# Decoder block with routed experts on one core: the row scatters of late attention steps issued one by one between GpSimd's splits and sums, or together

## The chip, the cores and the metric

The kernel runs on one core of a Trainium2 chip. The metric is the device time of one execution in microseconds (us). PE is the matrix engine (TensorE), DVE is VectorE, ACT is ScalarE, POOL is GpSimd, SP is the engine that only issues transfers. PSUM is the memory that PE writes its results to, SBUF the memory that all engines and the transfers share.

## What is computed

A post-norm decoder block over 16 sequences of 256 tokens with 256 features: self-attention with 16 heads, cross-attention on 120 context rows per sequence, and a mixture of 8 experts of which each token uses two. Cut to what matters:

```python
x = layernorm(x + self_attention(x))            # 16 heads of 16, ALiBi bias
x = layernorm(x + cross_attention(ctx, x, mask))
x_flat = x.reshape(4096, 256)
probs = softmax(x_flat @ gate_w.T)
topk_probs, topk_idx = top_k(probs, 2)
hidden = relu(einsum('th,ehf->tef', x_flat, w1) + b1)
all_out = einsum('tef,efh->teh', hidden, w2) + b2
y = sum(gathered(all_out, topk_idx) * topk_probs)
x = layernorm(x + y)
```

## The kernel before

It has two parts, each a block in which every engine has its own instruction queue, run in order; engines wait for one another on counting semaphores only.

**attention()** goes through software-pipelined steps i = -1 to 17 (B = 16 sequences). In step i the engines work on self-attention of sequence i (quarters u = 0 to 3 for scores, one group of four heads each), on cross-attention of sequence i - 1 (u = 4 to 7), and on projections, output products and router logits of neighbours, put by a fixed table into gaps between the groups. For every group PE writes scores (L718 for self-, L735 for cross-attention), DVE takes their negated row maxima (L866, L871) and splits them into bf16 parts (L913, L917), PE turns these (L748), DVE copies the result (L884, L891) into rows of `q_stack` or `cq_stack`, and PE computes the scores again with the maxima in them (L766, L774), whose exponentials ACT takes (L1156, L1160). Scores need operands as three bf16 parts. ACT makes the fp32 projection and its first part (L1108, L1143); POOL's `split` (L1227) makes the other two in three instructions (L1232, L1233, L1235); SP writes the parts to DRAM (d_q, d_k, d_cq, d_ck) and reads them back, spread over partitions, into the stacks (L491, L502).

**POOL in a step** (L1249) does, in this order: the split of q of sequence i + 1, of cq of i - 1, of k of i + 1; the normalising factors of cross-attention (`deviations`, L1243 to L1247) of i - 2; the sum `x1bo` (L1264); the split of ck of i; the sum `xbo` (L1273), which DVE reads when it adds the output product of self-attention (L942); in steps 11 to 15 five row scatters; and the factors of self-attention of i, which wait for DVE's mean and variance (L951).

**The scatters** bring each token's row of 260 floats to its place in the list of an expert in DRAM (`d_rows`). `send_rows` (L274 on; the indirect DMA is at L280) sends one tile of 128 tokens for one of its two choices per call of the DMA: 64 in all. Sequences 0 to 6 are routed in steps 9 and 10, which gives 28 scatters: five in each of steps 11 to 15, three at the start of step 16. The other 36 follow in steps 16 and 17 and behind them. Each scatter waits for the positions ("posu") and for its rows ("wr_x2").

**experts()** then works through 71 blocks of 128 rows and ends with the last layer norm.

In steps 9 to 16 ("halve") DVE (L975) and ACT (L1181) also turn the experts' weights into two fp16 halves, which SP loads and stores.

Of the kernel before, what the change touches and what calls it, by code (L numbers as in the profile page):

```python
# [18 lines left out]
B, L, D = 16, 256, 256  # L19
# [254 lines left out]
def send_rows(pool, sem, rt, XS, r, first, count):  # L274

    pool.wait_ge(sem("posu"), r + 1)
    for n in range(first, first + count):
        t, k = ROUTES[r][0] + n // 2, n % 2
        pool.wait_ge(sem("wr_x2"), 32 * (t // QT + 1))
        pool.indirect_dma_start(XS, bass.IndirectOffsetOnAxis(ap=rt["posu"][:, k, t:t + 1], axis=0),  # L280
                                rt["X2R"][:, t, :], None).then_inc(sem("scatter"), 16)


def attention(nc, ctx, ap, outer, sem):

    ident, identb, mhalf, LG, X2R, SC, b1c, dW, XS, YS, fill, rt = (outer[n] for n in (
        "ident", "identb", "mhalf", "LG", "X2R", "SC", "b1c", "dW", "XS", "YS", "fill", "rt"))
# [80 lines left out]
    def on(b):  # L368
        return not isinstance(b, int) or 0 <= b < B

    def wait(eng, name, val):
        if not isinstance(val, int) or val > 0:
            eng.wait_ge(sem(name), val)

    def wait_apart(eng, name, val, held, count):
        if not isinstance(val, int) or val > 0:
            apart(nc, eng, sem(name), val, (sem(held), count))
# [826 lines left out]
    @block.gpsimd  # L1204
    def _(pool):
        chain = Chain(pool, sem("pool_chain"), nc, (sem("ones"), 3))
        pool.memset(V[:, :, :, :], 1.0).then_inc(sem("ones"), 1)
        pool.memset(CV[:, :, :], 1.0).then_inc(sem("ones"), 1)
        pool.memset(mhalf[:, :], -0.5).then_inc(sem("ones"), 1)
        pool.memset(minus[:, QT:QT + 1], 0.0).then_inc(sem("minus"), 1)  # L1210
        pool.memset(minus[:, 0:QT], -1.0).then_inc(sem("minus"), 1)
        pool.wait_ge(sem("ones"), 3)
        pool.wait_ge(sem("minus"), 2)

        def route_constants():

            widths = [n for n in range(TMAX + 1) if f"keep{n}" in rt]
            pool.memset(rt["ones"][:, :], 1.0).then_inc(sem("ones_r"), 1)
            for n in widths:
                pool.memset(rt[f"keep{n}"][:, :, :], 1.0).then_inc(sem("ones_r"), 1)  # L1220
            pool.wait_ge(sem("ones_r"), 3)
            for n in widths:
                pool.memset(rt[f"keep{n}"][:, :, 0:1], 0.0).then_inc(sem("ones_r"), 1)
            pool.wait_ge(sem("ld_route"), 64)
            pool.tensor_copy(X2R[:, :, D + 2], rt["ids"][:, :]).then_inc(sem("ones_r"), 1)

        def split(n, b):  # L1227

            if not on(b):
                return  # L1230
            wait(pool, f"part0_{n}", b + 1)
            chain(pool.tensor_tensor(rest[n][:, :, :], full[n][:, :, :], part[n][:, :, 0, :], ALU.subtract))  # L1232
            chain(pool.tensor_tensor(part[n][:, :, 1, :], rest[n][:, :, :],  # L1233
                                     minus[:, 2:3].unsqueeze(1).to_broadcast([P, KT, width[n]]), ALU.add))
            pool.tensor_tensor(part[n][:, :, 2, :], rest[n][:, :, :], part[n][:, :, 1, :], ALU.subtract  # L1235
                               ).then_inc(sem(f"parts_{n}"), 1)

        def deviations(c, b):

            if not on(b):  # L1240
                return
            wait_apart(pool, f"mv{c}", QT * (b + 1), "ones", 3)
            chain(pool.tensor_scalar(ve[:, :], mv[:, :, 1], EPS, None, ALU.add))  # L1243
            ins = pool.tensor_tensor(rstd[:, :], ve[:, :], mhalf[:, 0:QT], ALU.pow)
            chain(ins)
            chain(pool.tensor_tensor(shift[:, :], mv[:, :, 0], rstd[:, :], ALU.mult))
            pool.tensor_tensor(shift[:, :], shift[:, :], minus[:, 0:QT], ALU.mult).then_inc(sem(f"rstd{c}"), 1)  # L1247

        def step(i, mode):  # L1249
            if i == B:  # L1250
                send_rows(pool, sem, rt, XS, 0, 25, 3)
            split("q", i + 1)
            split("cq", i - 1)
            if mode == "scale":
                pool.wait_ge(sem("wm"), 1)
                pool.partition_all_reduce(wg[:, :], wm[:, :], P, bass.bass_isa.ReduceOp.max
                                          ).then_inc(sem("wg"), 1)
            if not (isinstance(i, int) and i < 0):
                split("k", i + 1)
            deviations("c", i - 2)  # L1260
            if on(i - 1):
                wait(pool, "x1", i)
                wait(pool, "read_Oc", i - 1)
                pool.tensor_tensor(x1bo[:, :, :], x1s[:, :, :],  # L1264
                                   rows_b[:, 3, :].unsqueeze(1).to_broadcast([P, QT, D]), ALU.add
                                   ).then_inc(sem("x1bo"), 1)
            split("ck", i)
            if on(i):
                if isinstance(i, int) and i == 0:
                    pool.wait_ge(sem("ld_rows"), 64)  # L1270
                wait(pool, "ld_x", 16 * (i + 1))
                wait(pool, "read_O", i)
                pool.tensor_tensor(xbo[:, :, :], xrow[:, :, :],  # L1273
                                   rows_b[:, 1, :].unsqueeze(1).to_broadcast([P, QT, D]), ALU.add
                                   ).then_inc(sem("xbo"), 1)
            if i == 2:
                route_constants()
            if 11 <= i < B:
                send_rows(pool, sem, rt, XS, 0, 5 * (i - 11), 5)
            elif i == B:  # L1280
                send_rows(pool, sem, rt, XS, 1, 0, 24)
            elif i == B + 1:
                send_rows(pool, sem, rt, XS, 1, 24, 4)
                send_rows(pool, sem, rt, XS, 2, 0, 4)
            deviations("", i)

        for i in range(-1, B + 2):
            step(i, "scale" if i == 8 else None)
        send_rows(pool, sem, rt, XS, 3, 0, 4)
# [443 lines left out]
```

## Time and profile before

| | |
|---|---|
| median of 3 runs | 1307.39 us (1307.11, 1307.39, 1311.61) |
| profiled execution, whole | 1302.24 us |
| its span, first to last instruction | 1300.40 us |
| mean granted TensorE clock | 0.938 |
| busy: PE, DVE, ACT, POOL | 84%, 75%, 44%, 38% of the span |
| scatters into d_rows (L280) | 64, 65.1 us busy on POOL, 1017 ns each |
| DMA, mean | 149 GB/s, 194.03 MB |

The spans of engines are busy time, not work on the path that ends last; an engine with idle time can still hold the others up by coming late at one place. The attention steps fill the first 800 us of the span, the expert blocks nearly all of the rest. The durations below come from the profiled execution, which is 5.15 us shorter than the median. In a timeline each row is: start, duration, engine, line, operation, what it writes and reads, and in brackets the idle time of the engine just before it with what ended it.

### The profile page before, as it was taken

What the parts mean: (1) busy time and instruction counts of PE and PEld (TensorE: products, weight loads), DVE (VectorE), ACT (ScalarE), POOL (GpSimd) and SP (SyncE); (2) the same over time, 40 slices, a digit from 0 to 9 for tenths busy, and PEclk for the clock granted to TensorE, in tenths of its full rate; (3) what the DMA queues carried; (4) which work ended last, traced back from release to release, by engine and by line L of the source; (5) the groups of instructions that cost most, each with busy time, mean ns of one, the idle gap of its engine ahead of it and who ended that gap; (6) DMA issues with size and microseconds to landing.
All of it is one profiled execution on the core that took longest, in us unless ns stands there. A gap on an engine that the chain in (4) does not pass through costs nothing. (4 is left out here: it accounts for less than half of the span.)

```text
span 1300.4 us, 32359 instructions
## 1 busy us (share of the span) xinstructions
PE 1085.9 (84%) x9894; PEld 772.9 (59%) x9895; DVE 972.2 (75%) x2213; ACT 567.5 (44%) x1025; POOL 488.6 (38%) x603
## 2 busy tenths in 40 slices
PE   3778998999898888989888671899999999999970
PEld 2445666666665566656565441777777777777650
DVE  1668888888887889888887653677777787777754
ACT  1435555555554666676666420222323232223225
POOL 1334344334433534555653573122232223222224
PEclk7889999999999999999999755999999999999995
DMA  8476866785647688779986576742222222222228
GB/s 199 125 176 167 204 131 182 175 212 122 175 112 166 156 239 241 189 216 271 256 209 205 173 267 234 282 122 41 41 44 41 44 45 41 44 41 42 45 30 262
DMA packets 153670, 194.03 MB, mean 149 GB/s; under 512 B 30636, under 2 KB 133948, under 8 KB 149323
## 3 DMA queue, kind: packets, MB, share of 16 engines
q1 hardware_dynamic: 138568, 174.14, 49.9%
q0 software_dynamic: 13296, 17.83, 8.1%
q10 hardware_dynamic: 1728, 1.06, 0.4%
q8 instruction: 44, 0.72, 0.2%
q14 instruction: 34, 0.28, 0.1%
HBM read 122.63 MB, written 66.16 MB: 145 GB/s over the span
## 5 line engine op out<-in xcount | busy, mean ns | idle before, releaser
L1436 PE MATMUL HB<-xhi,W 128*128 128x128 f16 x2272 | 292.7, 221 | 21.2 <-issue 16.6
L1436 PEld LDWEIGHTS HB<-xhi,W 128*128 x2272 | 202.1, 98 | 66.2 <-issue 47.7
L1642 POOL DMA_INDIRECT d_sums<-ysc,tok x71 | 110.8, 1560 | 332.9 <-ACT ysc L1502 214.1
L1436 PE MATMUL HB<-xlo,W 128*128 128x128 f16 x1136 | 225.2, 220 | 0.0
L866 DVE TENSOR_REDUCE peaks<-SA 128x4 f32<-128x1024 f32 x128 | 156.6, 1224 | 65.5 <-PE SA L718 65.1
L1156 ACT ACTIVATE PT<-SB 128x1024 f32<-128x1024 f32 x128 | 131.1, 1024 | 119.3 <-PE SB L766 116.9
L1436 PEld LDWEIGHTS HB<-xlo,W 128*128 x1136 | 112.0, 99 | 49.7
L1558 DVE SCALAR_TENSOR_TENSOR hlo<-HB,hhi 128x512 f16<-128x512 f32 x142 | 98.2, 691 | 55.4 <-ACT hhi L1494 51.6
L1494 ACT ACTIVATE hhi<-HB 128x512 f16<-128x512 f32 x142 | 84.2, 593 | 119.6 <-DVE HB L1550 119.5
L1502 ACT ACTIVATE ysc<-yb,wv 128x256 f32<-128x256 f32 x71 | 36.1, 508 | 191.9 <-DVE yb L1582 189.1
L1550 DVE SCALAR_TENSOR_TENSOR HB<-HB,SC,b1c 128x512 f32<-128x512 f32 x142 | 107.1, 754 | 13.6 <-PE HB L1436 7.7
L1447 PE MATMUL YP<-W,hhi 128*128 x288 | 109.1, 380 | 0.6 <-DVE yb L1582 0.5
L1447 PE MATMUL R<-W,hhi 128*128 x280 | 106.1, 380 | 1.0
L766 PE MATMUL SB<-q_stack,k_stack 111*128 111x256 bf16 x512 | 78.4, 276 | 32.4 <-DVE q_stack L891 21.3
L718 PE MATMUL SA<-k_stack,q_stack 99*128 99x256 bf16 x512 | 79.5, 278 | 24.8 <-DMA k_stack<-d_k 18.3
L1160 ACT ACTIVATE PT<-SB 120x1024 f32<-120x1024 f32 x64 | 65.1, 1018 | 59.0 <-PE SB L774 58.9
L766 PEld LDWEIGHTS SB<-q_stack,k_stack 111*128 111x128 bf16 x512 | 46.5, 98 | 55.1 <-issue 26.4
L871 DVE TENSOR_REDUCE peaks<-SA 128x8 f32<-128x960 f32 x64 | 73.6, 1149 | 2.3 <-PE SA L735 2.2
L718 PEld LDWEIGHTS SA<-k_stack,q_stack 99*128 99x128 bf16 x512 | 48.7, 101 | 43.5 <-issue 20.0
L280 POOL DMA_INDIRECT d_rows<-X2R,posu x64 | 65.1, 1017 | 21.0 <-issue 18.2
L792 PE MATMUL AV<-PT,V 128*32 128x256 f32 x1024 | 69.3, 388 | 0.9 <-DVE ao L900 0.9
L1446 PE MATMUL YP<-W,hlo 128*128 x252 | 68.8, 273 | 0.0
(205 smaller groups left out, 2373.7 us busy)
## 6 DMA issues: line engine op xcount, KB each, us to landing
wst<-in_w SPq DMA_DIRECT2D x32, 1024.0 KB, 9.8
d_w<-w SPq DMA_DIRECT2D x16, 1024.0 KB, 8.4
W<-d_w SPq DMA_DIRECT2D x16, 1024.0 KB, 7.1
k_stack<-d_k SPq DMA_DIRECT2D x96, 128.0 KB
XB<-d_rows SPq DMA_DIRECT2D x65, 130.0 KB
d_q<-q_part SPq DMA_DIRECT2D x16, 384.0 KB, 5.8
d_k<-k_part SPq DMA_DIRECT2D x16, 384.0 KB, 2.7
q_stack<-d_q SPq DMA_DIRECT2D x16, 384.0 KB, 4.6
```

The costliest lines, as they stand in the source:

```text
L718: mm = pe.matmul(SA[:, j, t * L:(t + 1) * L], stack["q"][0:PROD + PARTS, h, t * P:(t + 1) * P], stack["k"][0:PROD + PARTS, h, :], start=Tr ...
L766: mm = pe.matmul(SB[:, j, k * L:(k + 1) * L], stack["k"][:, h, k * P:(k + 1) * P], stack["q"][:, h, :], start=True, stop=True)
L792: mm = pe.matmul(AV[32 * j:32 * j + 32, 0:L], V[:, k, h, :], PT[:, slot, j, k, :], start=(k == 0), stop=(k == QT - 1))
L866: dve.tensor_reduce(peaks[:, u % 2, :, 3 + 2 * half:5 + 2 * half].rearrange("p t j -> p j t"), SA[:, :, :].rearrange("p j (t n) -> p j t n ...
L871: dve.tensor_reduce(peaks[:, u % 2, :, 3:3 + GH].rearrange("p t j -> p j t"), SA[:, :, 0:4 * LC].rearrange("p a (c n) -> p a c n", n=LC), ...
L1156: act.activation(PT[:, slot, 2 * half:2 * half + 2, :, :].rearrange("p j k n -> p (j k n)"), SB[:, :, :].rearrange("p j n -> p (j n)"), AC ...
L1436: mm = pe.matmul(out, w.rearrange("p e n -> p (e n)"), x[n % 2][:, k, :], start=(k == 0 and half == 0 and x is xhi), stop=(k == KT - 1 and ...
L1447: mm = pe.matmul(YP[n % 2][:, :], hhi[n % 3][:, f, :], w, start=(f == 0), stop=(f == FT - 1))
L1494: act.activation(hhi[n % 3][:, 4 * c:4 * c + 4, :].rearrange("p f n -> p (f n)"), HB[n % 2][:, c, :], ACT.Relu).then_inc(sem("hhi"), 1)
L1550: dve.scalar_tensor_tensor(bank, bank, SC[:, 3:4], b1c[:, bass.ds(e, 1), 4 * c:4 * c + 4].rearrange("p e f -> p (e f)") .unsqueeze(2).to_b ...
L1558: dve.scalar_tensor_tensor(hlo[n % 3][:, 4 * c:4 * c + 4, :].rearrange("p f n -> p (f n)"), HB[n % 2][:, c, :], 0.0, hhi[n % 3][:, 4 * c:4 ...
L1642: pool.indirect_dma_start(YS, bass.IndirectOffsetOnAxis(ap=tok[n % 6][:, 0:1], axis=0), ysc[n % 2][:, :], None, compute_op=ALU.add).then_i ...
```

## The change

In steps 11 to 15 the five scatters are no longer issued in a row behind `xbo`. One goes out behind the q split, one behind the cq split, one ahead of the ck split, one behind it, ahead of `xbo`, and one behind `xbo`. Which rows each scatter sends, their order among themselves and their number are the same, as are the scatters of steps 16 and 17. Each call of `send_rows` begins with the wait for "posu", so there are four such waits more in each of the five steps.

```diff
--- before.py
+++ after.py
@@ -1249,8 +1249,14 @@
         def step(i, mode):
             if i == B:
                 send_rows(pool, sem, rt, XS, 0, 25, 3)
+            def one(n):
+                if 11 <= i < B:
+                    send_rows(pool, sem, rt, XS, 0, 5 * (i - 11) + n, 1)
+
             split("q", i + 1)
+            one(0)
             split("cq", i - 1)
+            one(1)
             if mode == "scale":
                 pool.wait_ge(sem("wm"), 1)
                 pool.partition_all_reduce(wg[:, :], wm[:, :], P, bass.bass_isa.ReduceOp.max
@@ -1264,7 +1270,9 @@
                 pool.tensor_tensor(x1bo[:, :, :], x1s[:, :, :],
                                    rows_b[:, 3, :].unsqueeze(1).to_broadcast([P, QT, D]), ALU.add
                                    ).then_inc(sem("x1bo"), 1)
+            one(2)
             split("ck", i)
+            one(3)
             if on(i):
                 if isinstance(i, int) and i == 0:
                     pool.wait_ge(sem("ld_rows"), 64)
@@ -1275,9 +1283,8 @@
                                    ).then_inc(sem("xbo"), 1)
             if i == 2:
                 route_constants()
-            if 11 <= i < B:
-                send_rows(pool, sem, rt, XS, 0, 5 * (i - 11), 5)
-            elif i == B:
+            one(4)
+            if i == B:
                 send_rows(pool, sem, rt, XS, 1, 0, 24)
             elif i == B + 1:
                 send_rows(pool, sem, rt, XS, 1, 24, 4)
```

## Rows read from the trace of the kernel before

**Rows 1.** the page's 40 slices: TensorE's granted clock, tenths, 32.5 us each

```profile
PEclk7889999999999999999999755999999999999995
```

**Rows 2.** busy time of each engine in step 12; then clock, DMA share, GB/s

```profile
550.00:593.00 43.00, 38.80 (x326) 26.74 (x325) 37.13 (x82) 28.16 (x49) 23.48 (x28) 1.00 0.84 228
```

**Rows 3.** timeline of POOL, late step 12: start, duration, [idle before, releaser]

```profile
583.02 1.05 POOL L1235 TENSOR_TENSOR ck_part<-ck_rest,ck_part 128x240 bf16<-128x240 f32 x1
584.02 1.27 POOL L1273 TENSOR_TENSOR xbo<-xrow,rows_b 128x512 f32<-128x512 f32 x1
585.47 1.08 POOL L280 DMA_INDIRECT d_rows<-X2R,posu  x1 [0.17 <-issue]
592.98 0.63 POOL L1243 TENSOR_SCALAR ve<-mv 128x2 f32<-128x2 f32 x1 [1.20 <-DVE mv L951]
```

**Rows 4.** timeline of POOL, the splits of steps 11 and 12

```profile
518.20 1.29 POOL L1232 TENSOR_TENSOR cq_rest<-cq_full,cq_part 128x512 f32<-128x512 f32 x1 [1.43 <-ACT cq_part L1143]
561.28 1.30 POOL L1232 TENSOR_TENSOR cq_rest<-cq_full,cq_part 128x512 f32<-128x512 f32 x1 [1.72 <-ACT cq_part L1143]
572.14 1.27 POOL L1232 TENSOR_TENSOR k_rest<-k_full,k_part 128x512 f32<-128x512 f32 x1 [7.08 <-ACT k_part L1143]
581.51 0.64 POOL L1232 TENSOR_TENSOR ck_rest<-ck_full,ck_part 128x240 f32<-128x240 f32 x1 [2.47 <-ACT ck_part L1143]
```

**Rows 5.** timeline of DVE, late step 12

```profile
584.53 0.69 DVE L927 TENSOR_TENSOR V<-BK,rows_b 128x512 f32<-128x512 f32 x1 [0.97 <-PE BK L634]
585.55 0.42 DVE L891 COPY cq_stack<-mts 15x1024 bf16<-15x1024 bf16 x1
588.84 0.65 DVE L891 COPY cq_stack<-mts 15x1024 bf16<-15x1024 bf16 x1
```

**Rows 6.** timeline of PE, late step 12 and early step 13

```profile
586.12 0.62 PE L774 MATMUL SB<-cq_stack,ck_stack 111*120 111x256 bf16 x4 [0.28 <-DVE cq_stack L891]
597.67 0.63 PE L643 MATMUL BK<-ident,x1s 128*128 128x128 f32 x4 [0.17 <-ACT x1s L1130]
```

**Rows 7.** timelines of POOL and DVE: two overlaps, in step 12 and step 15

```profile
557.23 1.04 POOL L1233 TENSOR_TENSOR q_part<-q_rest,minus 128x512 bf16<-128x512 f32 x1
557.29 1.26 DVE L891 COPY q_stack<-mts 15x1024 bf16<-15x1024 bf16 x1
712.98 1.26 POOL L1273 TENSOR_TENSOR xbo<-xrow,rows_b 128x512 f32<-128x512 f32 x1
713.92 0.60 DVE L891 COPY cq_stack<-mts 15x1024 bf16<-15x1024 bf16 x1
```

**Rows 8.** POOL in the expert blocks: timeline of a scatter; the groups of casts

```profile
841.37 1.58 POOL L1642 DMA_INDIRECT d_sums<-ysc,tok  x1 [4.22 <-ACT ysc L1502]
842.39 0.77 POOL L1633 CAST tok<-XH 128x1 uint32<-128x1 f32 x1
...
L1633 POOL CAST tok<-XH 128x1 uint32<-128x1 f32 x6 | 2.1, 384 | 14.6 <-DMA XH<-d_rows 14.6
```

**Rows 9.** timeline of PE: the scores of cross-attention in steps 11 and 12

```profile
532.28 0.59 PE L735 MATMUL SA<-ck_stack,cq_stack 99*128 99x120 bf16 x8 [0.95 <-DMA cq_stack<-d_cq]
533.23 0.60 PE L766 MATMUL SB<-q_stack,k_stack 111*128 111x256 bf16 x4 [0.35 <-DVE q_stack L891]
576.31 0.60 PE L766 MATMUL SB<-q_stack,k_stack 111*128 111x256 bf16 x4 [1.47 <-DVE q_stack L891]
```

**Rows 10.** the page's software DMA queue; busy time and DMA share, step 12

```profile
q0 software_dynamic: 13296, 17.83, 8.1%
...
565.00:567.90 2.90, 2.90 (x33) 2.02 (x26) 2.38 (x6) 2.28 (x4) 0.06 (x1) 1.00 0.49 136
585.00:599.00 14.00, 13.03 (x108) 9.04 (x105) 12.75 (x33) 8.18 (x15) 7.52 (x10) 1.00 1.05 285
```

**Rows 11.** transfers of the whole run: KB each, median us to landing

```profile
d_cq<-cq_part SPq DMA_DIRECT2D x16, 384.0 KB, 2.8
d_rows<-X2R,posu POOLq DMA_INDIRECT x64, 5.2
```

## The prediction

> **What bounds the kernel now.** I began with the clock, because a change of level would swamp everything else here. In the slices that hold steps 11 to 15 (the 16th to the 22nd figure, up to 715 us) the granted clock stands at nine tenths or more, its upper level of 2.4 GHz [rows 1], and the window of step 12 alone shows 1.00 [rows 2]; the clock takes no part in what follows. Next the busy time of one step. A full step is 43.00 us long; PE works 38.80 of them and DVE 37.13, ACT 28.16 and POOL only 23.48 [rows 2]. PE and DVE hand work to each other group by group, so a step is as long as that pair's alternating chain, and the other engines matter only where they make one of these two wait. The chain that ended last cannot be used: the profile follows it back only to about 710 us, behind the steps in question. So the argument goes by timelines. The reader should see three things in them: where POOL sits idle, what it is doing at the moment in which DVE wants the same kind of access, and what PE waits for.
>
> At the end of a step five scatters run in a row on POOL and then the self-attention deviations (L1243) wait for DVE's mean and variance. In step 12 POOL still idles 1.20 us there after the last scatter [rows 3]. Steps 11, 13, 14 and 15 repeat it with 0.90, 1.19, 1.19 and 0.87 us. The burst is thus hidden already, though closely, and taking it away from that place saves nothing by itself.
>
> **The change, part by part.** Nothing is removed: 25 scatters with 1.08 us for the first of a group [rows 3] stay, and 20 more waits on "posu" are met at once, since that semaphore has stood since step 10. What moves is the place of each.
>
> Scatter 0 goes between the q and the cq split. In step 12 the cq split starts at 561.28, when ACT is ready, after 1.72 us of idling, so the q split ended at 559.56 [rows 4]; with the gap of 0.17 and the 1.08 us of a first scatter [rows 3] the scatter ends at 560.81. Covered by 0.47 us; steps 13 and 14 are alike. In step 11 the idle time is 1.43 [rows 4], which leaves 0.18. Step 15 has no q split and idles longer. Cost 0; if a following instruction needs a scatter's usual gap, 0.1 in step 11.
>
> Scatter 1, before the k split, lies in 7.08 us of idling [rows 4]. Scatter 2, before the ck split, lies in 2.47 us of waiting for ACT [rows 4], in the other steps 2.46 to 2.85. Scatter 4 takes the place of the old first one. All cost 0 on POOL.
>
> Scatter 3, between the ck split and the xbo sum, is the one I price. Nobody waits for xbo that early (its reader, L942, comes some 5 us later), but the sum moves to a place where it meets a DVE copy. In step 12 the ck split ends at 583.02 + 1.05 = 584.07; plus 0.17 and 1.08 gives 585.32 as the new start of xbo, and 585.32 + 1.27 = 586.59 its end [rows 3]. DVE reaches its copy of the maxima into cq_stack (L891) at 585.55 [rows 5], inside that span. What such a meeting does is in the trace: a copy of this line that starts 0.06 us behind a POOL sum takes 1.26 instead of 0.42 us and ends at 558.55, which is 0.28 after the sum's end at 558.27; the one of step 15 meets xbo, takes 0.60 and ends at 714.52, again 0.28 after 714.24 [rows 7]. So the copy would end at 586.59 + 0.28 = 586.87 rather than 585.97: **+0.90 us**. PE is already waiting there: L774 starts at 586.12 after 0.28 us of waiting for this copy [rows 6]. From there PE runs without a pause through the Q item of step 13, and the T1 item at 597.67 follows Q through ACT, on which PE waits 0.17 us [rows 6], so the 0.90 goes through into the next step. Copy minus old start of xbo is 1.53 us here, and 1.52, 1.52 and 1.42 in steps 11, 13 and 14, against a shift of xbo of 1.25: the same meeting four times, 4 x 0.90 = 3.6 us. In step 15 the copy (713.92) comes ahead of the new start of xbo (712.98 + 1.25 = 714.23) and is freed of its present overlap: 0.42 - 0.60 = -0.18 us.
>
> That term hangs on 0.23 us. From below, if an instruction behind a scatter starts as late as the next scatter does (0.3 us after it), the copy goes first and the term is 0. Against this stands the trace's only pair of the kind: behind a scatter of the expert blocks the cast starts 842.39 - 841.37 = 1.02 us after it, not after its 1.58 us, so nothing is added to the dispatch; I take 0.90. The same pair gives the upper end: that cast takes 0.77 us against 0.38 for one that follows no scatter [rows 8]. With 0.39 more on xbo a step would lose 1.29, four 5.2 us.
>
> The Trainium skill, "SBUF — State Buffer", section "Who interferes with whom", says that VectorE's copy in a 2-port mode and a GpSimd instruction lock one shared port pair, and whoever issued first keeps it for its whole length. The overlaps above agree with it, 1.26 against 0.42 us. By this rule the sum is as above; by the page's "no contention otherwise" view of TensorE and ScalarE nothing else would slow down.
>
> The scatters' old neighbours gain a little: the second copy of step 12, which ran during a scatter, takes 0.65 instead of 0.42 us [rows 5]. The moved scatters miss it, 0.23 us of DVE in three steps, but PE does not wait for that copy; 0, at best -0.7.
>
> The transfers move too. Scatter 1 now starts its writes just as d_cq is written and cq_stack read. The software queue took 8.1% of 16 engines over 1300 us for 135 indirect transfers [rows 10], so 0.8 us of every DMA engine each. In 565.0 to 567.9, when d_cq is written, the DMA share is 0.49 [rows 10], so there is room: between 0 and 0.8 us of delay. Its cover is PE's wait for q_stack right behind the cross scores: 1.47 us in step 12, 0.35 in step 11, where the scores wait 0.95 us for cq_stack already [rows 9]; 1.47, 0.89 and 0.75 in steps 13, 14 and 15. At 0.4 us almost nothing comes through; I take 0, upper end 0.5 in all. Relief for the saturated end of the step [rows 10] gives 0, as neither PE nor DVE waits for a transfer there.
>
> **Sum.** 3.6 - 0.2 + 0 + 0 = +3.4 us. The profiled execution took 1302.24 us (span 1300.40), so it would take 1305.6. It lies 5.15 us below the median of the three runs, 1307.39, which would become **1310.8**. That is 0.26%, and a measurement of this kernel can tell about 0.5% (6.5 us) from no change.
>
> **Rivals.** (a) The copy goes first, or the shift is absorbed: 0 to -0.9 us, 1307.0. For it: only 0.23 us decide, and DVE idles 0.97 us just ahead [rows 5]. Against it: the cast behind a scatter. (b) Slower beyond 0.5%: scatter 1 stands in front of d_cq. If d_cq lands only when the scatter does, at the scatters' median of 5.2 us instead of 2.8 [rows 11], cq_stack is 2.4 us late; beyond the cover that is 2.05 + 0.93 + 0.93 + 1.5 + 1.65 = 7.1 us. It decides from 0.35 us of lateness in step 11 and from 1.47 in step 12. Against it: a DMA share of 0.49. Alone it gives 1314.5, with the meetings 1317.9. (c) Faster: the DMA engines are at a share of 1.05 from 585 to 599 us [rows 10]; spread scatters might bring DVE's and PE's inputs sooner. No wait of those two shows such an input, so even 1.3 us in each of five steps, 1300.9, is far-fetched. (d) The order of the instructions does not change in effect, because POOL waits anyway: 1307.4; the queue is in order, so this is unlikely.
>
> **How the numbers follow.** Forecast (+2 to +6 us) 0.52, (a) 0.26, (b) 0.14, (c) 0.06, (d) 0.02. The bounds of the forecast's terms run from -0.9 to +5.7, that is 1306.5 to 1313.1; the three runs spread over 4.5 us, and some of (b) has to be held, so the range is 1304.0 to 1316.0. Slower by over 0.5% is (b), 0.14; faster by over 0.5% is (c), 0.06; within 0.5% is the rest, 0.80.
>
> **What would show it.** In steps 11 to 14 of the changed kernel: L891's copy at the third quarter of the step near 1.3 us, xbo starting under 1.5 us after the ck split's end, L774's wait near 1.2 us, and each step close to 0.9 us longer. The cq split should start 1.4 to 1.8 us after the q split as now, and the deviations should idle some 4 us instead of 1.2. If L891 stays at 0.42 while xbo starts after it, (a) holds; if PE waits 1 us or more for cq_stack in each step, (b). The prediction is wrong if the meetings happen and the step is no longer, or if PE or DVE turns out to wait for something that the burst had held back.

## The result, and the profile after

The changed kernel takes 1314.2 us in the median of ten runs (1311.6 to 1317.59). The kernel before took 1307.0 in ten runs beside it (1301.74 to 1311.61). The ratio is 1.006 [1.0041, 1.008]: slower by 0.4 to 0.8%, some 8 us where 3.4 were forecast. The profiled execution took 1312.93 us, its span is 1311.1, against 1302.24 and 1300.4 before.

The page of the profile tells little. It is the share of busy time and the granted clock in 40 slices:

```profile
PE 1083.5 (83%) x9894; PEld 770.7 (59%) x9895; DVE 978.0 (75%) x2213; ACT 566.9 (43%) x1025; POOL 489.0 (37%) x603
PEclk7799999999999999999999765899999999999995
```

PE worked no more than before (1083.5 us against 1085.9), and DVE's 978.0 us are 5.8 more than its 972.2. The clock's figures for steps 11 to 15 are nines as in [rows 1], up to 721 us; a dip of a few microseconds doesn't show at 33 us a figure.

The place of the loss shows when steps are measured. DVE starts the addition of xbo (L942) once per step; from one such start to the next is one step. All these lengths, in us, are differences of starts in the timelines of DVE:

| step | 11 | 12 | 13 | 14 | 15 | sum |
|---|---|---|---|---|---|---|
| before | 42.92 | 43.28 | 43.11 | 42.93 | 42.38 | 214.62 |
| after | 47.74 | 43.78 | 43.78 | 43.71 | 47.46 | 226.47 |

The difference is 11.85 us: 4.82 in step 11, 0.50, 0.67 and 0.78 in steps 12 to 14, 5.08 in step 15. (This execution had begun step 11 by 1.18 us earlier, which leaves the 10.7 us by which the spans differ.) Four different things are in it: a meeting of a sum and a copy in every step, a stall in step 11, the clock behind both, and a part of step 15 that comes and goes without any change.

**Steps 12 to 14: the forecast meeting.** First the busy time of the engines in the stretch that answers to [rows 2] (PE, PEld, DVE, ACT, POOL; then clock, DMA share, GB/s), then the timelines of POOL, DVE and PE in the late step 12 (start, duration, what, idle time before and who ended it):

```profile
553.40:597.10 43.70, 38.84 (x326) 26.75 (x324) 38.29 (x82) 28.14 (x49) 23.97 (x27) 1.00 0.86 244
...
586.65 0.64 POOL L1235 TENSOR_TENSOR ck_part<-ck_rest,ck_part 128x240 bf16<-128x240 f32 x1
587.44 1.26 POOL L280 DMA_INDIRECT d_rows<-X2R,posu  x1 [0.15 <-issue]
588.73 1.28 POOL L1281 TENSOR_TENSOR xbo<-xrow,rows_b 128x512 f32<-128x512 f32 x1
597.13 0.63 POOL L1243 TENSOR_SCALAR ve<-mv 128x2 f32<-128x2 f32 x1 [5.98 <-DVE mv L951]
...
583.91 0.62 DVE L891 COPY cq_stack<-mts 15x1024 bf16<-15x1024 bf16 x1
588.35 0.69 DVE L927 TENSOR_TENSOR V<-BK,rows_b 128x512 f32<-128x512 f32 x1 [0.51 <-PE BK L634]
589.37 0.93 DVE L891 COPY cq_stack<-mts 15x1024 bf16<-15x1024 bf16 x1
590.45 0.62 PE L774 MATMUL SB<-cq_stack,ck_stack 111*120 111x256 bf16 x4 [0.78 <-DVE cq_stack L891]
```

PE's work, 38.84 us, and the clock are those of [rows 2]; DVE's work is 1.16 us more, in a window that is 0.70 us longer. The copy L891 starts 0.64 us behind the start of xbo and ends at 590.30, which is 0.29 after xbo's end at 590.01. It takes 0.93 instead of the 0.42 of [rows 5], and PE waits 0.78 us for it instead of the 0.28 of [rows 6]. The step is longer by as much, 0.50. A smaller meeting stands ahead of it: the scatter before the ck split runs from 582.84 to 584.30, beside DVE's previous copy into cq_stack, which takes 0.62 us (583.91) instead of 0.42, and the L774 that reads it waits 0.62 instead of 0.42. Kernels below with the first three scatters moved and no meeting of xbo (a3, b2, c2) show what these three cost together: some 0.17 us in each of steps 13 and 14. The deviations idle 5.98 us where they idled 1.20 [rows 3], and nothing gains by it.

**Step 11: a stall of POOL that was not foreseen.** POOL's timeline around the first scatter, PE's row of the cross scores, and three windows of 2 us behind them:

```profile
514.44 1.16 POOL L1235 TENSOR_TENSOR q_part<-q_rest,q_part 128x512 bf16<-128x512 f32 x1 [0.43 <-POOL q_part L1233]
519.62 1.31 POOL L280 DMA_INDIRECT d_rows<-X2R,posu  x1 [4.03 <-issue]
520.97 1.17 POOL L1232 TENSOR_TENSOR cq_rest<-cq_full,cq_part 128x512 f32<-128x512 f32 x1
...
534.00 0.98 PE L735 MATMUL SA<-ck_stack,cq_stack 99*128 99x120 bf16 x8 [3.42 <-DMA cq_stack<-d_cq]
...
533.00:535.00 2.00, 1.00 (x10) 0.94 (x11) 0.00 (x0) 0.00 (x0) 1.71 (x4) 0.75 1.13 333
535.00:537.00 2.00, 2.00 (x16) 0.89 (x18) 1.92 (x4) 1.02 (x1) 1.13 (x2) 0.50 0.28 88
537.00:539.00 2.00, 2.00 (x20) 1.28 (x12) 0.26 (x1) 0.38 (x1) 0.00 (x0) 0.90 0.14 46
```

The q split ends at 515.60. The first scatter of the kernel starts only at 519.62, after 4.03 us in which POOL waited for nothing that the profile shows. In the kernel before, the first scatter, behind xbo, idled 0.20 us (542.41). So the cq split starts at 520.97, d_cq is written late, and the cross scores of PE wait 3.42 us for cq_stack where they waited 0.95 [rows 9]. From the end of this idling at 534.0 to 537.4 the granted clock is 0.50, its lower level of 1.2 GHz. The meeting of xbo and the copy is in step 11 as well: the copy at 545.26 takes 1.25 us and PE's L774 at 546.66 waits 1.11 us for it.

**Step 15: the meeting, with the other sign and much dearer.** Timelines of POOL, DVE and PE, and windows of 2 us; last, a window of the kernel before:

```profile
720.26 0.98 POOL L280 DMA_INDIRECT d_rows<-X2R,posu  x1 [0.16 <-issue]
721.28 1.27 POOL L1281 TENSOR_TENSOR xbo<-xrow,rows_b 128x512 f32<-128x512 f32 x1
721.01 1.84 DVE L891 COPY cq_stack<-mts 15x1024 bf16<-15x1024 bf16 x1
720.29 0.44 PE L806 MATMUL AV<-ident,avs 128*128 128x128 f32 x2 [1.01 <-ACT avs L1170]
722.99 1.08 PE L774 MATMUL SB<-cq_stack,ck_stack 111*120 111x256 bf16 x4 [1.39 <-DVE cq_stack L891]
...
719.00:721.00 2.00, 0.99 (x13) 0.80 (x13) 1.01 (x3) 1.85 (x4) 1.77 (x2) 1.00 0.85 195
721.00:723.00 2.00, 0.61 (x8) 0.40 (x5) 1.96 (x2) 0.60 (x1) 1.81 (x3) 0.68 1.02 380
723.00:725.00 2.00, 2.00 (x12) 0.86 (x12) 1.93 (x5) 0.83 (x1) 0.70 (x1) 0.50 1.14 306
729.00:731.00 2.00, 2.00 (x18) 1.23 (x17) 1.19 (x4) 0.41 (x1) 0.00 (x0) 1.00 0.04 8
...
682.20:685.60 3.40, 3.25 (x18) 2.02 (x19) 1.77 (x5) 1.94 (x5) 0.00 (x0) 0.50 1.12 373
```

The copy's record starts at 721.01, while the scatter runs (to 721.24). Then xbo goes ahead of it, from 721.28 to 722.55, and the copy ends at 722.85: 1.84 us instead of 0.60 [rows 7]. PE idles 1.39 us ahead of L774, from 721.60 to 722.99, and from 721.7 to 728.5 the clock is granted at 0.50. L774 takes 1.08 us where it takes 0.62 at the upper level. The clock fell here when this wait had only just begun, 1.4 us behind an earlier one of 1.01 us which the kernel before has too (1.02 at 713.21), so this profile alone doesn't show that the meeting brought it down. All of them together do: in the four profiles with the meeting (after, b1, a2, c1) the clock falls at this place, in b1, a2 and c1 0.1 to 0.4 us behind PE's wait for the copy, and in none of the ten without it.

Not all of the 5.08 us is the change's. The kernel before has a stretch at 0.50 in this step as well, from 682.2 to 685.6, behind a wait of PE of 1.75 us (L718 at 681.51). In the changed kernel that stretch is twice as long, 687.6 to 694.4, and so it is in the kernel before when it was profiled again (a1), whose step 15 is 1.13 us longer.

### The profile page after: what moved, and what is told of

Read it like the earlier page. It is cut to its first block and busy times, and to the rows that moved or that the text cites. A ratio compares the mean times of both kernels' runs of the same rounds, so it can differ in the third digit from the quotient of the medians.

```text
span 1311.1 us, 32379 instructions
## 1 busy us (share of the span) xinstructions
PE 1083.5 (83%) x9894; PEld 770.7 (59%) x9895; DVE 978.0 (75%) x2213; ACT 566.9 (43%) x1025; POOL 489.0 (37%) x603
## 5 line engine op out<-in xcount | busy, mean ns | idle before, releaser
L718 PE MATMUL SA<-k_stack,q_stack 99*128 99x256 bf16 x512 | 80.6, 281 | 26.9 <-DMA k_stack<-d_k 20.8
L718 PEld LDWEIGHTS SA<-k_stack,q_stack 99*128 99x128 bf16 x512 | 49.1, 102 | 45.5 <-issue 22.2
```

Source lines behind the costliest of these rows:

```text
L718: mm = pe.matmul(SA[:, j, t * L:(t + 1) * L], stack["q"][0:PROD + PARTS, h, t * P:(t + 1) * P], stack["k"][0:PROD + PARTS, h, :], start=Tr ...
```

## The experiments

The kernels were run in three groups, each group with runs of the kernel before between them: 29 (median 1305.99), 24 (1304.33) and 23 (1304.42). A ratio is to those, with its 95% interval; it is worked out from all fast runs and isn't the quotient of two medians. The kernel before spreads from 1297 to 1312 us over all of them, so single executions tell by their traces, not by their times. Lengths of steps 11 to 15 in each profiled execution:

| kernel | 11 | 12 | 13 | 14 | 15 | ratio |
|---|---|---|---|---|---|---|
| a1, before again | 42.93 | 44.89 | 43.11 | 42.91 | 43.51 | one run |
| a2, third alone | 44.15 | 44.04 | 44.03 | 43.94 | 45.05 | 1.0038 |
| a3, all but third | 47.70 | 44.70 | 43.29 | 43.10 | 43.39 | 1.0017 |
| a4, first of step 11 | 48.13 | 43.11 | 43.11 | 42.93 | 42.48 | 1.0032 |
| b1, after again | 49.48 | 43.80 | 45.54 | 43.72 | 44.77 | 1.0074 |
| b2, xbo waits | 47.64 | 44.70 | 43.28 | 43.11 | 43.24 | 1.0035 |
| b3, sums moved | 44.57 | 43.09 | 43.09 | 42.88 | 42.44 | 1.007 |
| b4, first in step 10 | 43.12 | 43.11 | 43.11 | 42.90 | 42.39 | one run |
| c1, after, padded | 43.63 | 43.78 | 45.54 | 43.93 | 44.65 | 1.0024 |
| c2, xbo waits, padded | 43.13 | 44.67 | 43.27 | 43.10 | 43.21 | 1.002 |
| c3, first in step 12 | 42.93 | 44.90 | 43.10 | 42.92 | 43.51 | one run |
| c4, behind the cq split | 43.12 | 44.73 | 43.11 | 42.91 | 43.47 | one run |

In the kernels of experiments `one(p)` stands at the five places (0 behind the q split, 1 behind the cq split, 2 ahead of the ck split, 3 behind it, 4 behind xbo) and sends every scatter of the step whose place is p:

```diff
+            def one(p):
                 if 11 <= i < B:
+                    places = [0, 1, 2, 3, 4]
+                    for n in range(5):
+                        if places[n] == p:
+                            send_rows(pool, sem, rt, XS, 0, 5 * (i - 11) + n, 1)
```

With these numbers it is the changed kernel; below only `places` is given where no more is changed.

**a1: the kernel before once more**, to see what a step does by itself.

> The kernel before once more, for a second profile of it. Every theory expects the first profile to repeat: steps 11 to 14 of 42.9 to 43.3 us and step 15 of about 42.4 us, the first scatter of step 11 with under 0.5 us of idling ahead of it, and the granted clock at its upper level from 686 to 721 us. If a step of this second profile is 3 us longer or shorter than in the first, differences of that size between single profiles mean nothing.

It took 1307.09 us. Two steps differ from the first profile of the same kernel: step 12 by +1.61 and step 15 by +1.13. PE's rows of step 12, and windows of 2 us:

```profile
575.52 0.59 PE L735 MATMUL SA<-ck_stack,cq_stack 99*128 99x120 bf16 x8 [0.49 <-DMA cq_stack<-d_cq]
576.92 0.60 PE L766 MATMUL SB<-q_stack,k_stack 111*128 111x256 bf16 x4 [0.81 <-DVE q_stack L891]
...
576.00:578.00 2.00, 1.19 (x15) 0.69 (x16) 1.94 (x5) 0.57 (x2) 1.71 (x4) 0.91 0.28 81
578.00:580.00 2.00, 2.00 (x16) 1.01 (x8) 1.93 (x4) 0.97 (x2) 1.51 (x3) 0.50 0.41 117
```

PE idles 0.49 and 0.81 us within 2 us, and the clock is at 0.50 in the window behind. Where it was profiled first, the same place shows PE waiting 0 and then 1.47 us [rows 9] at full clock. So some 1.6 us in step 12 (in b1 and c1 in step 13) and 1 us in step 15 come and go with the execution: all six profiles with a long step 12 (a1, a3, b2, c2, c3, c4) have 43.2 to 43.5 us in step 15, and the kernels without a meeting and without a long step 12 (before, a4, b3, b4) have 42.4 to 42.5. The first six have the long stretch of low clock early in step 15 (6.8 us), the other four the short one (3.4 us). So it was expected wrongly that the clock would be at its upper level from 686 us on: in a1 it is at 0.50 from 683.4 to 690.3. Differences of that size in one profile are not put down to an edit below.

**a2: a scatter only ahead of xbo**, the other four behind it.

```diff
+                    places = [3, 4, 4, 4, 4]
```

> One scatter of each late step goes ahead of xbo, the other four stay in a row behind xbo. Theory A (the copy into cq_stack has to wait for the moved xbo sum, and in step 15 for longer, upon which TensorE idles and its clock falls): 0.5 to 0.9 us longer in each of steps 11 to 14, 3 to 5 us in step 15, in all 6 to 8 us or 0.5 to 0.6% over the kernel before. Rival B (the loss is in the stall of 4 us ahead of the first early scatter and in the transfers beside d_cq): no more than 3 us, since neither is in this kernel.

1308.96 us, ratio 1.0038 [1.0018, 1.0059]. Timelines of POOL, DVE and PE, late step 12:

```profile
586.50 1.28 POOL L1284 TENSOR_TENSOR xbo<-xrow,rows_b 128x512 f32<-128x512 f32 x1
586.70 1.37 DVE L891 COPY cq_stack<-mts 15x1024 bf16<-15x1024 bf16 x1
588.22 0.62 PE L774 MATMUL SB<-cq_stack,ck_stack 111*120 111x256 bf16 x4 [1.23 <-DVE cq_stack L891]
```

With only this scatter moved, the meeting is as priced: the copy takes 1.37 us and PE waits 1.23, 0.95 more than in [rows 6]. Steps 11 to 14 are longer by 1.23, 0.76, 0.92 and 1.01 us, 3.9 in all where 3.6 were forecast, and step 15 by 2.7, 6.6 us together. No stall: the first scatter idles 0.20 us. By the time alone the run decides less: the ratio stands for 5.0 us, but the medians differ by 3.0, and up to 3 had been allowed to rival B. It is the rows that speak for the meeting.

**a3: all moved but the one ahead of xbo**, which stays behind it.

```diff
+                    places = [0, 1, 2, 4, 4]
```

> The counterpart: scatters 0, 1 and 2 are spread as in the changed kernel, 3 and 4 stay behind xbo. Theory A: the copy keeps 0.42 us in step 12 and step 15 keeps about 42.4 us; what is left is the stall of 4 us in step 11, of which 3.4 us reach TensorE, so 3 to 4.5 us over the kernel before. Rival B: nearly all of the 7 us, as both of its causes are here.

1307.22 us, ratio 1.0017 [1.0, 1.0035]. The copy takes 0.42 us in step 12 and 0.61 in step 15, so without the third scatter there is no meeting. The loss in step 11 stays (47.70), with this row of POOL:

```profile
519.99 1.31 POOL L280 DMA_INDIRECT d_rows<-X2R,posu  x1 [3.34 <-issue]
```

Scatters 1 and 2 stand beside d_cq here as in the changed kernel. Steps 13 and 14 are some 0.17 us longer than in the kernel before, and steps 12 and 15 are like those of a1. This speaks against rival (b). The ratio stands for 2.2 us, less than the 3 to 4.5 expected.

**a4: only the first scatter of step 11 behind the q split**, all else as in the kernel before.

```diff
+                    places = [0, 4, 4, 4, 4] if i == 11 else [4] * 5
```

> Only one scatter of the 25 moves: the first one of step 11 goes out behind the q split. If a scatter's first use costs a stall wherever POOL has not idled long enough ahead of it, the stall of 4 us appears here too and the kernel is 3 to 4.5 us slower than before. If the stall of the changed kernel's profile was a chance of one execution, this one is within 1 us of the kernel before and shows less than 0.5 us of idling ahead of that scatter.

1309.87 us, ratio 1.0032 [1.0012, 1.0051]. POOL's first scatter and PE's cross scores:

```profile
523.66 1.31 POOL L280 DMA_INDIRECT d_rows<-X2R,posu  x1 [4.55 <-issue]
538.53 0.59 PE L735 MATMUL SA<-ck_stack,cq_stack 99*128 99x120 bf16 x8 [3.91 <-DMA cq_stack<-d_cq]
```

One scatter out of 64, moved once, brings the 4.55 us of idling on POOL, 3.91 us of waiting on PE and a step 11 of 48.13 us. Steps 12 to 15 are those of the kernel before to 0.2 us.

**b1: the changed kernel again**, beside the next three.

> The changed kernel once more, on the same chip as the next two. Expected of every theory: 0.4 to 0.8% over the kernel before (5 to 10 us), and again about 4 us of idling ahead of the first scatter, the copy of about 0.93 us in steps 12 to 14 and of 1.8 us in step 15.

1314.32 us in eight runs, ratio 1.0074 [1.0048, 1.0101]. Its first scatter:

```profile
521.92 1.38 POOL L280 DMA_INDIRECT d_rows<-X2R,posu  x1 [3.74 <-issue]
```

**b2: the changed kernel, with xbo made to wait for the copy of the cross item.** The meeting is taken away without moving anything:

```diff
+                if 11 <= i < B:
+                    wait(pool, "auxc", NG * (i - 1) + 2)
                 pool.tensor_tensor(xbo[:, :, :], xrow[:, :, :],
```

> The changed kernel with one wait more: in steps 11 to 15 the xbo sum waits until DVE's copy into cq_stack (the one that it met) is done. Nothing else differs. Theory A (the meeting of the two is what costs): the copy is back at 0.42 us, steps 12 to 14 fall from 43.75 to about 43.2 us, step 15 keeps its clock until its end and falls to 42.4 to 43.9; all in all 4 to 6 us less than the changed kernel, leaving the stall of step 11. Rival B (transfers beside d_cq, or the stall alone): no difference, or slower, since only a wait was added.

1308.99 us, ratio 1.0035 [1.0014, 1.0056]. DVE, POOL and PE, late step 13:

```profile
632.73 0.42 DVE L891 COPY cq_stack<-mts 15x1024 bf16<-15x1024 bf16 x1
633.33 1.27 POOL L1283 TENSOR_TENSOR xbo<-xrow,rows_b 128x512 f32<-128x512 f32 x1 [1.28 <-DVE cq_stack L891]
633.29 0.62 PE L774 MATMUL SB<-cq_stack,ck_stack 111*120 111x256 bf16 x4 [0.27 <-DVE cq_stack L891]
```

The copy is back at 0.42 us and PE's wait at 0.27; step 13 is 43.28 long instead of the 43.78 of the changed kernel's first profile, and step 15 43.24 instead of 47.46 and 44.77 in its two. The wait costs POOL 1.28 us, and no step gets longer by it. b1 less b2 is 0.39% of the time, 5 us. Step 11 keeps its stall (3.31 us).

**b3: both sums moved to where DVE has no copy**, in the kernel before, in all steps, as an attempt at a version that beats it: xbo behind the cq split, x1bo behind the ck split, each held back until the copy near it has been read.

```diff
             split("cq", i - 1)
+            one(1)
+            if on(i):
...
+                wait(pool, "mparts", NG * i + 3)
+                pool.tensor_tensor(xbo[:, :, :], xrow[:, :, :],
...
             split("ck", i)
+            one(3)
+            if on(i - 1):
...
+                wait(pool, "auxc", NG * (i - 1) + 2)
+                pool.tensor_tensor(x1bo[:, :, :], x1s[:, :, :],
...
+            one(4)
```

with `places = [1, 3, 4, 4, 4]`.

> Built on the kernel before, to use the cause instead of suffering it: in all steps xbo goes behind the cq split and waits until DVE has split the maxima of group 2; x1bo goes behind the ck split and waits for the copy into cq_stack; the scatters of steps 11 to 15 stand one behind the cq split, one behind the ck split, three at the end. Theory A: DVE's L917, which takes 1.2 to 1.3 us in every full step because x1bo runs, takes 0.17, so up to 1.0 us less per step over some 14 steps, 5 to 14 us less than the kernel before (0.4 to 1.1%). If DVE's time there is not on the path, no change. Slower if xbo has to wait for its row load and the k split behind it comes late.

1312.82 us, ratio 1.007 [1.0046, 1.0093]: slower. DVE's rows of b3 in step 12 first, then those of the kernel before at the same place; last POOL in step 16, in b3 and before:

```profile
581.64 0.17 DVE L917 TENSOR_TENSOR peaks<-peaks 128x8 f32<-128x8 f32 x1
583.53 0.28 DVE L884 COPY mts<-MT 15x256 bf16<-15x256 bf16 x1 [1.04 <-PE MT L748]
...
577.79 1.28 DVE L917 TENSOR_TENSOR peaks<-peaks 128x8 f32<-128x8 f32 x1
579.68 0.28 DVE L884 COPY mts<-MT 15x256 bf16<-15x256 bf16 x1
...
755.11 1.26 POOL L1285 TENSOR_TENSOR x1bo<-x1s,rows_b 128x512 f32<-128x512 f32 x1 [8.57 <-DVE cq_stack L891]
744.26 1.26 POOL L1264 TENSOR_TENSOR x1bo<-x1s,rows_b 128x512 f32<-128x512 f32 x1
```

L917 took 1.28 us beside x1bo and takes 0.17 now; the microsecond goes into DVE's wait for PE (1.04 us for MT), and the step is 43.09 against 43.28. This overlap was off the path. In step 16 x1bo now waits 8.57 us for a copy, and the scatters behind it follow: x1bo starts 32.01 us behind the last L942 of step 15 (723.10) where it started 24.84 behind it before (719.42). Behind the last L942 the kernel then needs 586.2 us instead of 581.0. The other thirteen profiles need 578.5 to 582.8 us there, so 3.4 us or more of the loss is b3's own. The late x1bo of step 16 is its likely cause, which is argued and not shown: which of the later waits carries it is open. The longer step 11 (44.57 us) has no stall (0.20), but 3.4 us of clock at 0.50, from 536.0 on.

**b4: the first scatter of all at the end of step 10**, the second behind the q split of step 11, three at its end; steps 12 to 15 as before.

```diff
             split("q", i + 1)
+            if i == 11:
+                send_rows(pool, sem, rt, XS, 0, 1, 1)
...
             deviations("", i)
+            if i == 10:
+                send_rows(pool, sem, rt, XS, 0, 0, 1)
```

> Where does the stall ahead of the first early scatter belong? Scatter 0 goes out at the end of step 10, where POOL idles 3.5 us, scatter 1 behind the q split of step 11, the rest as before. If the first scatter of a run pays it, scatter 0 shows 3 to 5 us of idling ahead of it and scatter 1 under 0.5. If the place behind the q split of step 11 has it, scatter 1 shows it still.

1300.98 us in its one execution, within the spread of the kernel before. POOL's first two scatters:

```profile
508.91 1.30 POOL L280 DMA_INDIRECT d_rows<-X2R,posu  x1 [0.77 <-issue]
515.80 0.99 POOL L280 DMA_INDIRECT d_rows<-X2R,posu  x1 [0.15 <-issue]
```

The second one stands where the stall was and idles 0.15 us. The first idles 0.77 us in its new place. So it is neither every scatter behind the q split nor a fixed price of the first one, wherever it stands.

**c1 and c2: b1 and b2 with 48 waits on POOL in step 5** that are met long before. They do nothing but put all later instructions of POOL further on in its code.

```diff
+            if i == 5:
+                for n in range(24):
+                    pool.wait_ge(sem("ones"), 3)
+                    pool.wait_ge(sem("minus"), 2)
```

> The changed kernel with 48 waits that are always met, put into POOL's queue in step 5. They do no work; they only shift every later instruction of POOL to another position of its code. Theory P (the stall ahead of the first scatter comes from where in POOL's code that scatter lies, such as the end of a piece that is loaded): the stall of 3.3 to 4.6 us is gone or elsewhere, step 11 about 43.5 us, and the kernel 3 to 5 us faster than the changed one, +0.2 to +0.5% over the kernel before. Theory F (the first scatter of a run needs this time if it is issued at this point of the step): the stall stays and so does the loss of 0.6 to 0.75%.

> The same padding in the changed kernel whose xbo sum waits for the copy. Theory P: with the meetings and the stall both gone, nothing of the loss is left: within 0.15% of the kernel before, steps 11 to 14 of 43.0 to 43.3 us. Theory F: as without the padding, +0.35%.

c1 takes 1307.47 us, ratio 1.0024 [1.0, 1.0047]; c2 1306.53, 1.002 [0.9998, 1.0043]. The first scatters of c1, c2, c3 and c4 (below):

```profile
520.02 1.31 POOL L280 DMA_INDIRECT d_rows<-X2R,posu  x1 [0.20 <-issue]
...
516.82 1.31 POOL L280 DMA_INDIRECT d_rows<-X2R,posu  x1 [0.20 <-issue]
...
558.70 1.31 POOL L280 DMA_INDIRECT d_rows<-X2R,posu  x1 [0.20 <-issue]
...
521.39 1.31 POOL L280 DMA_INDIRECT d_rows<-X2R,posu  x1 [0.20 <-issue]
```

The stall is gone in both, step 11 is back at 43.63 and 43.13 us. c1 still has the meetings (copy of step 15: 1.84 us, step 44.65). c2 has neither, and its interval holds 1; its 0.2% is above the 0.15% expected, by less than the noise.

**c3: the first scatter behind the q split of step 12**, none in step 11, and **c4: the first scatter behind the cq split of step 11.** The rest follows at the ends of the steps.

```diff
             split("q", i + 1)
+            if 12 <= i < B:
+                send_rows(pool, sem, rt, XS, 0, 6 * (i - 12), 1)
```

```diff
+                    places = [1, 4, 4, 4, 4] if i == 11 else [4] * 5
```

> No scatter in step 11; the first of all goes out behind the q split of step 12, five at the end of steps 12 to 15, four at the start of step 16. Theory F: 3 to 5 us of idling ahead of that first scatter and a step 12 of about 47.5 us. Theory P: 0.2 us of idling and a step 12 of about 43.3 us.

> Only one scatter moves: the first of step 11 goes out behind the cq split, where POOL idles 7 us. Theory F: it shows a stall of 3 to 5 us which nobody waits for, step 11 stays at about 43 us. Theory P: no stall at that scatter, step 11 also about 43 us.

1305.1 and 1305.38 us in one execution each, no stall in either (0.20 us each), step 11 at 42.93 and 43.12 us.

**What the twelve say together.** The stall is in all five profiles in which the first scatter stands directly behind the q split of step 11 with the same code ahead of it (after, b1, a3, a4, b2: 3.31 to 4.55 us), and in none of the nine others (0.20 us in each but b4). The same scatter, at the same moment of the step, with 48 waits more ahead of it (c1, c2), behind another split (c4), one step on (c3) or as the second (b4) doesn't stall. So its place in POOL's code decides; that is shown.

The traces say more of that place. Where an instruction of a split or of the deviations waits for POOL's own one before, POOL idles 0.14 us, 221 times in the kernel before, and once 0.43. Here is that row of the kernel before, then its like in b4 and c1, and last the queue of kind "instruction" in the changed kernel, in the idle time from 515.6 to 519.62 us (packets, MB, share):

```profile
515.62 1.16 POOL L1235 TENSOR_TENSOR q_part<-q_rest,q_part 128x512 bf16<-128x512 f32 x1 [0.43 <-POOL q_part L1233]
...
513.28 1.06 POOL L1233 TENSOR_TENSOR q_part<-q_rest,minus 128x512 bf16<-128x512 f32 x1 [0.44 <-POOL q_rest L1232]
...
492.85 0.20 POOL L1246 TENSOR_TENSOR shift<-mv,rstd 128x2 f32<-128x2 f32 x1 [0.43 <-POOL rstd L1244]
...
q14 instruction: 2, 0.02, 1.5%
```

The row with 0.43 marks a fixed place in POOL's queue. In the kernel before, a1, a2, c3, c4 and the five kernels with the stall it is the last instruction of the q split of step 11. With a scatter more ahead of it (b4) it comes one instruction sooner, with 48 waits more (c1, c2) 27 us ahead of the first scatter. (In b3, where the sums are moved in all steps, the only such row is in step 13.) The stall befalls the scatter that comes directly behind the mark. In b4 a part of the split stands between the two, and neither it nor the scatter is held up.

Two packets of 8 KB of instructions fall into the idle time of all five stalls, and the scatter starts 1.6 to 2.4 us behind the start of the later one. But they are there without a stall too, some 2 to 4 us behind the mark, and b4's second scatter starts in the same moment as one of them (515.79). In c1 and c2 one of them has moved along and follows the mark by 0.7 us. That the stalled scatter waits for such a transfer is near at hand, and not shown: no row names what ends the wait. The Trainium skill, "Runtime: NRT & Kernel Launch", section "Instruction fetch mechanics", says that an engine's instructions come in blocks of 16 KiB, and that crossing from one to the next is mostly hidden. A crossing that isn't hidden would fit a stall that 48 extra waits remove, but 4.03 us is not what the page would lead one to expect, nor that a scatter is held up and a part of a split is not.

How the 0.6 to 0.7% divide is known only roughly. The meeting alone is 0.38% (a2), and it is 0.39% as b1 less b2 but 0.04% as c1 less c2. The stall alone is 0.32% (a4); it is 0.50% as b1 less c1 and 0.15% as b2 less c2, and a3 has it whole with 0.17%. Each ratio is sure to some 0.2% to either side, and a difference of two to some 0.3%. About 4 us for each is within the noise of all of them; closer than that the runs don't say.

## Why the prediction was right and wrong

**The burst was hidden already, and its going saves nothing: right.** The deviations' idle time grew from 1.20 to 5.98 us, and no step is shorter.

**Scatter 0 costs nothing: wrong**, one of the two great errors. The step reasoned from the cover behind the q split (0.18 us in step 11) and from the duration of a first scatter, and took the dispatch for granted; it left "0.1 in step 11" as its worst. The runs showed 3.3 to 4.6 us of idling ahead of it, in that one place of the code. With 0.18 us of cover almost all of it reaches PE, and the clock adds to it: step 11 +4.8, the meeting there included. The cover was misread too: the first scatter of the kernel takes 1.31 us in the trace of before (542.41), not 1.08, which leaves 1.43 - 0.17 - 1.31 = -0.05. The trace of before had no row of a scatter in this place. What it had was the thin cover and, in the row just ahead of the new place, the one idle time of 0.43 among 221 of 0.14. What that would cost a scatter nobody could read from it, but the step could have been priced as one that passes on whatever comes, with a bound well above 0.1. In steps 12 to 14 scatter 0 did cost nothing.

**Scatters 1, 2 and 4 cost nothing, and the transfers beside d_cq neither: right to 0.2 us a step.** a3 holds 0, 1 and 2 in their new places, and its steps 13 and 14 are some 0.17 us longer than before. A part of that is scatter 2, which now runs beside an earlier copy into cq_stack (0.62 us for 0.42); the prediction counted only the copy that is freed. The rival that scatter 1 delays d_cq fell with it: PE's late cq_stack in step 11 came from POOL's late split. The time which that rival gave, 1314.5, is close to the measured one, but its mechanism is not there.

**Scatter 3 makes xbo meet the copy, 0.90 us a step: the mechanism right, the size too high in the whole change.** a2 shows it bare: a copy of 1.37 us, PE's wait +0.95, 3.9 us over steps 11 to 14. The other condition, that a scatter adds nothing to the dispatch of the sum behind it, held as well: a2's sum starts 1.11 us behind the scatter, of which 1.08 is the scatter itself. In the changed kernel steps 12 to 14 lost only 0.50, 0.67 and 0.78. The term took the end of the ck split from before (its last part 1.05 us), but with scatter 2 ahead of it the last part takes 0.64 us, in a3 and b2 (steps 13 and 14) too. So xbo runs 0.4 us sooner against the copy, which has less left to wait. Each moved scatter changes the instructions behind it, and the term was worked out as if the others had stayed.

**Step 15, -0.18: wrong in sign.** The prediction had the copy (713.92) ahead of the new xbo (714.23) and thus free. In the changed kernel the copy did come first, 721.01 against 721.28, and was still served last, because the scatter ahead held it until 721.24 and xbo followed it within 0.04 us. That a scatter slows such a copy stood in the prediction's own rows (0.65 for 0.42 [rows 5]), and by its own sum the copy at 713.92 fell into scatter 3 (713.15 to 714.23), not into free time. The Trainium skill, "SBUF — State Buffer", section "Who interferes with whom", lets whoever issues first keep the shared ports; the order of the recorded starts here, 0.27 us the other way, was not the order in which the two were served. What made it dear is the clock at 0.50, next to PE's wait of 1.39 us. Over the profiles, step 15 is 45.48 us on average with the meeting (after, b1, a2, c1) and 43.00 without it (the other ten, both of before among them): +2.5. With the early stretch of low clock alike it is +4.0 to +4.3 for the changed kernel's first profile (47.46 against 43.2 to 43.5) and +2.2 to +2.7 for b1, a2 and c1 (44.65 to 45.05 against 42.4 to 42.5).

**"The clock takes no part": wrong.** It was read from slices of 32.5 us and from step 12, and not even of before is it true: there the clock is at 0.50 for 3.4 us in step 15. A wait that is added changes it further: in step 11 the granted clock fell to its lower level behind PE's long wait, in step 15 it fell in all four profiles with the meeting and in no other, and even the kernel before shows another stretch of it when it runs again (a1). The pauses of under 1 us in steps 12 to 14 passed without it.

**Sum and rivals.** In the profile of the changed kernel the meetings of steps 12 to 14 gave 1.95 us for the forecast's 2.7; step 11 gave 4.8 for 0.90, step 15 5.1 for -0.18. The median went up by 7 to 10 us, to 1314.2 and 1314.3. The range holds it, but through the room left for a rival that was not the cause: that is luck. The ratio lies beyond the 0.5% within which the prediction had put 0.80 of its chances. Rivals (a) and (d) fell by the copy's rows, (c) by a3 and c2, neither of which is faster than the kernel before. No version tried here beats it: the best ratios, a3's and c2's, are 0.2% above, and b3, which was meant to, is 0.7% above. b4's 1300.98, c3's and c4's are single executions inside its spread.

## What to carry to other kernels

An instruction that moves on an engine with idle time must be priced at its new place twice: by what it pushes against other engines (here a GpSimd sum against a VectorE copy, 0.95 us of PE's wait), and by how thin the cover there is, because a stall of 4 us whose size no row of before tells goes through nearly whole where there is next to no cover. If several instructions move together, work out the sequence anew from the first one on. An added wait of the matrix engine of a microsecond or more can bring a stretch of low clock that costs as much again, so a step that the clock left alone before is not safe from it; and a mean over 30 us doesn't show such a stretch. Before a profile's step is compared with another's, compare their stretches of low clock: two executions of one kernel differed by 1.6 us in a step by that alone.

## What the runs showed of the hardware

- A place in GpSimd's code where one scatter waits 3.31 to 4.55 us for nothing that the profile shows, in five of five profiles with the same code ahead of it; with 48 more waits ahead it waits 0.20. With the same code ahead of it the place is marked, in the kernel before too, by an idle time of 0.43 instead of 0.14 us at the instruction just ahead of it.
- A VectorE copy that is waiting for the shared access can be passed over: held by a scatter from 721.01 on, it ended 0.3 us behind a sum that started only at 721.28, and took 1.84 us instead of 0.42; the same in b1 and c1 (1.84) and a2 (1.94).
- The granted clock fell to 0.50 behind waits of PE of 3.42 us (after, step 11), 1.40 (b1 and c1, step 15), and 0.49 followed by 0.81 (a1), and in the changed kernel's step 15 0.1 us into a wait of 1.39 that followed one of 1.01; it did not fall behind single waits of 0.78 (after) and 1.23 (a2), nor behind the 1.47 of [rows 9].
- The kernel before showed two lengths of step 12 (43.3 and 44.9 us) and of step 15 (42.4 and 43.5) in its two profiled executions, a part of the 15 us over which its runs spread. The two lengths of step 15 go with 3.4 and 6.8 us of clock at 0.50.
